# Two buffers instead of three for half tiles of the adjacency, and longer rings of masks, in a two-layer graph network kernel

## The chip, the cores and the metric

The kernel runs on one core of one Trainium2 chip. The metric is the device time of one execution in microseconds (us), the median of several runs.

## What is computed

The input is x (8192 nodes by 64 channels, f32) and adj (8192 by 8192, int32, 256 MB). Two graph layers follow each other.

```
h = relu(layernorm(x))                      # layer 0: two attention passes, mask = adj > 0
for i in range(2):
    Wh = h @ W[i];  u, v = vectors made of Wh and the attention weights
    e = leaky_relu(u + v.T + c)
    att = softmax(where(mask, e, -9e15), axis=1)
    h = 0.2 * h_input + 0.8 * elu(att @ Wh)
x = x + concat(h_input, h1, h2) @ mlp_w + mlp_b
h = relu(layernorm(x))                      # layer 1: mean over the neighbours, a = (adj == 1)
x = x + concat(a @ h / rowsum(a), h) @ weight + bias
```

The softmax is computed without exponentials of the whole matrix: exp(leaky_relu(u+v)) splits into a product of a row factor and a column factor on either side of the kink. So each attention pass needs, for each element of the adjacency, one bit "neighbour, on-side" (u+v above zero) and one bit "neighbour, off-side", and multiplies these two bit masks with scaled values of Wh.

## The kernel before, in words

**Tiles.** The rows are taken in 8 groups of 1024 and the columns in 8 chunks of 1024; one (group, chunk) pair is a tile, number n, 64 in all. In the first attention pass a tile comes from HBM as two half tiles of 128 x 4096 int32, 2 MB each (line L285, issued by SyncE, short SP, from its own queue), number m = 2n + h. The landing places are `adjb`, NA buffers of 16 KB per partition, and SP issues load m only when VectorE (DVE) has converted half tile m - NA (`sp.wait_ge(coded, m - NA + 1)`).

**The front of a tile.** DVE converts each half tile to bytes (`convert`, L850), packs two bits per element (`pack_pairs` L860 and L861, `pack` L865), TensorE (PE) transposes the packed bytes (L1491), ScalarE (ACT) takes them out of PSUM into one of NP = 4 buffers `pt` (L469) and stores them to HBM as `codes_d` (L473, 256 KB). DVE converts tile n + 3 while it makes the masks of tile n.

**The units.** A tile is used in four units q = 0..3. For each unit ACT computes a sign ramp into the ring `onb` of NS buffers (L461, two instructions). DVE turns it in place into the on-side mask (`on_mask`, L828) and makes the off-side mask into the ring `offb` of NO buffers (`off_mask`, L838). PE multiplies: 16 matmuls with the on mask (L1501), then 16 with the off mask (L1507). ACT's ramp for unit U waits for PE's on-side matmuls and for the off mask of unit U - NS; DVE's off mask for unit U waits for PE's off-side matmuls of unit U - NO.

**The passes.** Pass 0 reads the adjacency itself. Pass 1 reads the 256 KB codes back, and so does the last stage, the neighbour mean, in which DVE picks masks out of the codes into the same ring `onb` (`pick`, L1333) and PE multiplies them (L1714). Every engine's program is one fixed list written out in order; the waits are semaphores.

**DVE's order in pass 0.** For a tile n with no side work it is: on 0, on 1, off 0, convert(n+3, 0), off 1, on 2, convert(n+3, 1), off 2, on 3, pack_pairs, off 3, pack. In the first eight tiles of the pass the splitting of Wh is interleaved; in the first four or so tiles of each later group the row work of the group before.

**The start.** SP issues the loads of x, the weights, and then the half tiles. Between the half tiles its queue holds the stores of m0 (eight of 256 KB, L288) at places given by the table `STORES`; each waits for the projection's products. POOL issues the small vectors' stores and their broadcasts (`u_d`, L325; `ub`, L332), the stored h (L338) and m1 (L355).

**The region.** All of the above but u shares one 94 KB region per partition: `adjb` at 0, `code`, `packed`, `pt`, `onb` and `offb` behind it. The m0 products wait for their store in the region's last 16 KB (78 to 94 KB), where mask buffers lie too, so the first user of such a buffer waits for `m0_st`: an ACT ramp (unit NS - 2) and DVE's first off mask.

Of the kernel before, what the change touches and what calls it, by code (L numbers as in the profile page):

```python
# [11 lines left out]
U8 = mybir.dt.uint8  # L12
# [14 lines left out]
CHJ = 1024  # L27
# [5 lines left out]
NG = N // RG  # L33
# [16 lines left out]
HTOP = 4096.0  # L50
ROOT = 0x5F3759DF
SPLIT_ON, SPLIT_OFF, SPLIT_Y = 5, 3, 3
NA, NP, NS, NO = 3, 4, 8, 6
KB = 1024


def word(bits):
    return bits * 0x01010101


def w32(buf):
    return buf.bitcast(U32)
# [24 lines left out]
def gnn_program(nc, x, adj, w, lin_w, lin_b, attn, mlp_w, mlp_b, w1, bias1, out):  # L87
    ctx = ExitStack()
    with ctx:
# [3 lines left out]
        def sem(name):  # L93
            return ctx.enter_context(nc.semaphore(name))
# [56 lines left out]
        def at(off, n, dt):  # L151
            return region[:, off:off + n].bitcast(dt)

        adjb = [at(16 * i * KB, 16 * KB, I32).rearrange("p (t j) -> p t j", j=CHJ) for i in range(NA)]
        code = at(48 * KB, 8 * KB, U8).rearrange("p (t j) -> p t j", j=CHJ)
        packed = at(56 * KB, 2 * KB, U8)
        pt = [at(58 * KB + 2 * i * KB, 2 * KB, U8) for i in range(NP)]
        onb = [at(66 * KB + 2 * i * KB, 2 * KB, U8) for i in range(NS)]
        offb = [at(82 * KB + 2 * i * KB, 2 * KB, U8) for i in range(NO)]
        xq = [at(78 * KB + 4 * ((k + 1) % 4) * KB, 4 * KB, FP32).rearrange("p (t c) -> p t c", c=C) for k in range(4)]  # L160
        m0 = [at(78 * KB + 2 * ((k + 2) % 8) * KB, 2 * KB, FP32).rearrange("p (t c) -> p t c", c=C) for k in range(NG)]
        xi = [at(2 * i * KB, 2 * KB, FP32).rearrange("p (t c) -> p t c", c=C) for i in range(2)]
# [63 lines left out]
        m0_st, m_st = sem("m0_stored"), [sem(f"m1_stored{i}") for i in range(2)]  # L226
# [27 lines left out]
        o_r, o_st = sem("out_ready"), [sem(f"out_stored{i}") for i in range(2)]  # L254

        NWA, NWT = 16 * 6, 16 * 8
        STORES = {3: (0,), 4: (1, 2), 5: (3,), 6: (4, 5, 6, 7)}

        def nth(l, c):

# [6 lines left out]
        with nc.Block() as block:  # L267

            @block.sync
            def _(sp):  # L270
# [9 lines left out]
                for m in range(2 * NT):  # L280
# [4 lines left out]
                    sp.dma_start(adjb[m % NA], adj_v[g, h, :, :, c * CHJ:(c + 1) * CHJ]).then_inc(adj_in[m % NA], 16)  # L285
                    for k in STORES.get(m, ()):
                        sp.wait_ge(mm_out, 3 * k + 3)
# [109 lines left out]
            def _(act):  # L397
# [45 lines left out]
                def ramps(l, n, q):  # L443
                    U = LU * l + 4 * n + q
                    g, c = n // NCH, n % NCH
                    G = NG * l + g
                    if U >= NS:
                        act.wait_ge(on_done, U - NS + 1)
                        act.wait_ge(off_r, U - NS + 1)
                    elif U == NS - 2:  # L450
                        act.wait_ge(m0_st, 16 * NG)
                    if q == 0 and c == 0:
                        act.wait_ge(ub_in[G % 2], 16 * (G // 2 + 1))
                    if q == 0 and g == 0 and l == 0:
                        act.wait_ge(bv_r, 1)
                    if q == 0 and g == 0 and l == 1:
                        act.wait_ge(d_r, NG + c + 1)
                    sv = onb[U % NS].rearrange("k (i b) -> k b i", b=2)
                    for b in range(2):
                        t = c * TC + 2 * q + b  # L460
                        last = nc.scalar.activation(sv[:, b, :], ub[G % 2][:, :], ACT.Relu, bias=bigv[l][:, t:t + 1], scale=BIG)  # L461
                    last.then_inc(sgn, 1)
# [63 lines left out]
                for n in range(NT):  # L526
                    g, r = n // NCH, n % NCH
                    ramps(0, n, 0)
                    if g == 0 and r > 0:
                        cast_high(0, r)  # L530
                    ramps(0, n, 1)
                    if n + 1 < NT:
                        take_codes(n + 1)
                    if r == 5 and g > 0:
                        high(NG + g - 1)
                    ramps(0, n, 2)
                    if n + 1 < NT:
                        store_codes(n + 1)
                    if g == 0 and r > 0:
                        cast_middle(0, r)  # L540
                    ramps(0, n, 3)
                    if g > 0 and r == 7:
                        products(NG + g - 1, 0, tpb)
                    if g > 1 and r < 2:
                        products(NG + g - 2, r + 1, tpb)
                    if g > 0 and r == 0:
                        scaled_sums(g - 1)
                    if g > 0 and r == 3:
                        row_exp(g - 1)
                    if g > 0 and r == 6:  # L550
                        take_ht(NG + g - 1, tpb)
# [32 lines left out]
            def _(dve):  # L584
# [246 lines left out]
                def off_mask(l, n, q):  # L831
                    U = LU * l + 4 * n + q
                    if U >= NO:
                        dve.wait_ge(off_done, U - NO + 1)
                    elif U == 0:
                        dve.wait_ge(m0_st, 16 * NG)
                    dve.wait_ge(on_r, U + 1)
                    nc.vector.scalar_tensor_tensor(w32(offb[U % NO]), w32(pt[(NT * l + n) % NP]), word(BITS[q]), w32(onb[U % NS]),  # L838
                                                   ALU.bitwise_and, ALU.bitwise_xor).then_inc(off_r, 1)
# [174 lines left out]
                for n in range(NT):  # L1014
# [5 lines left out]
                    on_mask(0, n, 0)  # L1020
                    on_mask(0, n, 1)
                    off_mask(0, n, 0)
                    if n + 1 < NCH:
                        split_rest(0, n + 1)
                    if ahead:
                        convert(n + 3, 0)
                    off_mask(0, n, 1)
                    if g > 0 and r == 1:
                        add_pairs(g - 1)
# [17 lines left out]
                    if n == 1:  # L1047
                        h_spread(0)
                    off_mask(0, n, 2)
                    if g > 0 and r == 1:  # L1050
                        lonely_add(g - 1)
# [733 lines left out]
```

## Time and profile before

| quantity | us |
|---|---|
| median of 3 runs | 1757.43 (1756.73 to 1758.02) |
| the profiled execution | 1757.3 |
| its span, first to last instruction | 1755.5 |
| PE busy in the span | 1532.0 (87%) |
| DVE busy | 1539.7 (88%) |
| ACT busy | 1269.0 (72%) |
| DMA queue of SP, share of 16 engines | 46.9% |

The busy times are unions over the whole span, and the stages differ: pass 0 ends at about 865 us, pass 1 at about 1500 us, and the mean takes the rest. The shares above say little of any one stage, so the rows below are cut by stage.

### The profile page before, as it was taken

How to read it: one execution, taken by the hardware profiler on the slowest of the kernel's cores; microseconds unless marked ns; L12 is line 12 of the kernel's file. 1: busy time of each engine (PE TensorE's matmuls, PEld its weight loads, DVE VectorE, ACT ScalarE, POOL GpSimd, SP SyncE). 2: the span in 40 equal slices, each digit the busy share in tenths (PEclk: the TensorE clock that was granted, in tenths of full speed). 3: DMA queues.
4: the chain of work that ended last, by engine and by line, in shares of the span. 5: the costliest groups of instructions: out<-in, count | busy, mean ns of one | idle time of the engine just before them, and what ended most of it. 6: DMA issues, size and time to landing. Idle time of an engine off the chain costs nothing. (4 is left out here: it accounts for less than half of the span.)

```text
span 1755.5 us, 50261 instructions
## 1 busy us (share of the span) xinstructions
PE 1532.0 (87%) x21779; PEld 1483.6 (85%) x21779; DVE 1539.7 (88%) x2544; ACT 1269.0 (72%) x1404; POOL 82.7 (5%) x116
## 2 busy tenths in 40 slices
PE   2268888888988888888779999999999999799998
PEld 2267778787878878787779999999999999799998
DVE  7799999999999999999788878879688788986665
ACT  4668888888979989888689999999999995000000
POOL 1100000101000010101010000000000000000000
PEclk9689999999999999999989999999999999999999
DMA  7998999999999999998121112122121211233231
GB/s 248 263 363 322 374 359 393 355 409 361 406 379 386 389 378 402 353 409 317 37 68 44 56 43 56 44 68 57 43 62 44 56 50 31 61 112 90 86 93 43
DMA packets 115389, 356.02 MB, mean 203 GB/s; under 512 B 9184, under 2 KB 17376, under 8 KB 115168
## 3 DMA queue, kind: packets, MB, share of 16 engines
q1 hardware_dynamic: 92192, 306.37, 46.9%
q0 software_dynamic: 8512, 27.33, 5.8%
q10 hardware_dynamic: 14464, 19.11, 3.0%
q8 instruction: 171, 2.80, 0.7%
q14 instruction: 50, 0.41, 0.1%
HBM read 325.45 MB, written 27.33 MB: 201 GB/s over the span
## 5 line engine op out<-in xcount | busy, mean ns | idle before, releaser
L461 ACT ACTIVATE region<-ub,bigv 128x1024 uint8<-128x1024 f32 x1024 | 1096.0, 1152 | 28.6 <-PE bank L1507 11.2
L1501 PE MATMUL bank<-wsplit,region 128*128 128x195 bf16 x8192 | 779.3, 248 | 46.2 <-DVE region L828 37.3
L1501 PEld LDWEIGHTS bank<-wsplit,region 128*128 128x128 fp8e3 x8192 | 687.1, 98 | 58.4 <-DVE region L828 41.3
L1507 PE MATMUL bank<-wsplit,region 128*128 128x130 f16 x8192 | 556.6, 221 | 63.4 <-DVE region L838 62.3
L1507 PEld LDWEIGHTS bank<-wsplit,region 128*128 128x128 fp8e3 x8192 | 499.0, 98 | 92.8 <-DVE region L838 92.7
L838 DVE SCALAR_TENSOR_TENSOR region<-region 128x512 uint32<-128x512 uint32 x512 | 338.4, 680 | 10.9 <-PE bank L1507 8.7
L828 DVE SCALAR_TENSOR_TENSOR region<-region 128x512 uint32<-128x512 uint32 x512 | 334.2, 681 | 10.8 <-ACT region L461 10.7
L850 DVE TENSOR_SCALAR region<-region 128x4096 uint8<-128x4096 int32 x128 | 292.0, 2281 | 9.6 <-DMA region<-in_adj 9.6
L1714 PE MATMUL bank<-wsplit,region 128*128 128x129 f16 x4096 | 243.5, 222 | 11.2 <-DVE region L1333 11.2
L1714 PEld LDWEIGHTS bank<-wsplit,region 128*128 128x128 fp8e3 x4096 | 241.4, 99 | 12.4 <-DVE region L1333 12.4
L1333 DVE TENSOR_SCALAR region<-region 128x512 uint32<-128x512 uint32 x256 | 100.2, 424 | 43.2 <-PE bank L1714 37.4
L469 ACT ACTIVATE region<-bank 128x1024 uint16<-128x1024 uint16 x64 | 66.0, 1031 | 26.8 <-PE bank L1491 26.0
L493 ACT ACTIVATE po<-po 128x512 f32<-128x512 f32 x16 | 10.0, 626 | 85.3 <-DVE po L946 85.3
L1491 PE MATMUL bank<-identb,region 128*128 128x128 bf16 x512 | 40.6, 224 | 33.9 <-DVE region L865 23.3
L1491 PEld LDWEIGHTS bank<-identb,region 128*128 128x128 bf16 x512 | 32.4, 100 | 34.5 <-DVE region L865 23.7
L1459 PE MATMUL bank<-w,hT 128*128 128x130 f16 (+2 forms) x512 | 37.5, 224 | 19.8 <-ACT hT L418 9.5
L1459 PEld LDWEIGHTS bank<-w,hT 128*128 128x128 f16 x512 | 30.9, 103 | 22.1 <-issue 9.8
L325 POOL DMA_DIRECT2D u_d<-vu x16 | 12.1, 760 | 671.8 <-DVE vu L660 608.0
L1322 DVE SCALAR_TENSOR_TENSOR region<-region 128x512 uint32<-128x512 uint32 x64 | 43.6, 682 | 0.0
L860 DVE SCALAR_TENSOR_TENSOR region<-region 128x512 uint32<-128x512 uint32 x64 | 43.5, 679 | 0.1
L865 DVE SCALAR_TENSOR_TENSOR region<-region 128x512 uint32<-128x512 uint32 x64 | 43.5, 679 | 0.0
L861 DVE SCALAR_TENSOR_TENSOR region<-region 128x512 uint32<-128x512 uint32 x64 | 43.4, 679 | 0.0
(192 smaller groups left out, 689.8 us busy)
## 6 DMA issues: line engine op xcount, KB each, us to landing
region<-in_adj SPq DMA_DIRECT2D x128, 2048.0 KB, 10.8
region<-codes_d SPq DMA_DIRECT2D x128, 256.0 KB, 2.7
codes_d<-region ACTq DMA_DIRECT2D x64, 256.0 KB, 6.4
ub<-u_d POOLq DMA_DIRECT2D x16, 512.0 KB, 6.1
hg<-h_d POOLq DMA_DIRECT2D x16, 256.0 KB, 6.2
stg<-m_d POOLq DMA_DIRECT2D x16, 256.0 KB, 5.0
region<-in_x SPq DMA_DIRECT2D x4, 512.0 KB, 6.8
h_d<-wsplit POOLq DMA_DIRECT2D x4, 512.0 KB, 4.4
```

The lines of the kernel that those rows point to most:

```text
L461: last = nc.scalar.activation(sv[:, b, :], ub[G % 2][:, :], ACT.Relu, bias=bigv[l][:, t:t + 1], scale=BIG)
L469: nc.scalar.activation(pt[n % NP].bitcast(U16), tpb[:, :].bitcast(U16), ACT.Copy).then_inc(p_in, 1)
L828: nc.vector.scalar_tensor_tensor(on, on, word(BITS[q]), w32(pt[(NT * l + n) % NP]), ALU.bitwise_and, ALU.bitwise_and).then_inc(on_r, 1)
L838: nc.vector.scalar_tensor_tensor(w32(offb[U % NO]), w32(pt[(NT * l + n) % NP]), word(BITS[q]), w32(onb[U % NS]), ALU.bitwise_and, ALU.bitw ...
L850: nc.vector.tensor_scalar(code[:, 4 * h:4 * h + 4, :], adjb[m % NA], 1.375, 3.0, ALU.mult, ALU.min).then_inc(coded, 1)
L1322: nc.vector.scalar_tensor_tensor(w32(xb[i % 2]), m32, 1, m32, ALU.logical_shift_right, ALU.bitwise_xor).then_inc(mixed, 1)
L1333: nc.vector.tensor_scalar(w32(onb[V % NS]), w32(xb[i % 2]), word(BITS[q]), None, ALU.bitwise_and).then_inc(eq, 1)
L1459: last = nc.tensor.matmul(pb[:, k * width:(k + 1) * width], ht[:, it * P:(it + 1) * P], rhs(j), start=(k == 0 and j == 0), stop=(j == 1), ...
L1491: last = nc.tensor.transpose(tpb[:, :].bitcast(BF16)[:, it * P:(it + 1) * P], src[:, it, :], identb[:, :])
L1501: return nc.tensor.matmul(acc_on[it], columns(onb[U % NS], it, b), wsplit[:, c * TC + 2 * q + b, 0:WC], start=(c == 0 and q == 0 and b == ...
L1507: return nc.tensor.matmul(acc_off[it], columns(offb[U % NO], it, b), woff[:, c * TC + 2 * q + b, WO:WO + WF], start=(c == 0 and q == 0 and ...
L1714: last = nc.tensor.matmul(acc_m[g % 2][it], columns(onb[V % NS], it, b), wf16[:, c * TC + 2 * q + b, :], start=(first and b == 0 and it % ...
```

## The change

`adjb` gets two buffers in place of three, which frees 16 KB per partition. The ring of on-side masks grows from 8 to 12 buffers and that of off-side masks from 6 to 10. The region is laid out anew, and what hangs on the number of buffers moves with it: SP's load m waits for the conversion of m - 2; the m0 stores stand one load earlier in SP's queue; the wait for these stores leaves ACT's ramp and goes from DVE's off mask 0 to off mask 2, the first whose buffer lies in the m0 area. No instruction that computes is added or removed.

```
-NA, NP, NS, NO = 3, 4, 8, 6
+NA, NP, NS, NO = 2, 4, 12, 10
...
-        code = at(48 * KB, 8 * KB, U8).rearrange("p (t j) -> p t j", j=CHJ)
-        packed = at(56 * KB, 2 * KB, U8)
-        pt = [at(58 * KB + 2 * i * KB, 2 * KB, U8) for i in range(NP)]
-        onb = [at(66 * KB + 2 * i * KB, 2 * KB, U8) for i in range(NS)]
-        offb = [at(82 * KB + 2 * i * KB, 2 * KB, U8) for i in range(NO)]
+        code = at(32 * KB, 8 * KB, U8).rearrange("p (t j) -> p t j", j=CHJ)
+        packed = at(40 * KB, 2 * KB, U8)
+        pt = [at(42 * KB + 2 * i * KB, 2 * KB, U8) for i in range(NP)]
+        onb = [at(50 * KB + 2 * i * KB, 2 * KB, U8) for i in range(NS)]
+        offb = [at(74 * KB + 2 * i * KB, 2 * KB, U8) for i in range(NO)]
...
-        STORES = {3: (0,), 4: (1, 2), 5: (3,), 6: (4, 5, 6, 7)}
+        STORES = {2: (0,), 3: (1, 2), 4: (3,), 5: (4, 5, 6, 7)}
...
                     if U >= NS:
                         act.wait_ge(on_done, U - NS + 1)
                         act.wait_ge(off_r, U - NS + 1)
-                    elif U == NS - 2:
-                        act.wait_ge(m0_st, 16 * NG)
...
                     if U >= NO:
                         dve.wait_ge(off_done, U - NO + 1)
-                    elif U == 0:
+                    elif U == 2:
                         dve.wait_ge(m0_st, 16 * NG)
```

## Rows read from the trace of the kernel before

**Rows 1.** Windows: busy us per engine, PEclk, DMA share, GB/s; pass 0, pass 1.
```profile
98.00:833.00 735.00, 621.44 (x8334) 580.82 (x8332) 734.25 (x924) 628.25 (x734) 28.09 (x25) 0.99 0.97 374
1000.00:1400.00 400.00, 400.00 (x5715) 400.00 (x5713) 319.58 (x598) 376.36 (x353) 20.87 (x30) 1.00 0.18 53
```
**Rows 2.** Waits in 98 to 833: us in total, times, longest.
```profile
PE bank L1507 <- DVE region L838: 60.4, 80, 1.9
PE bank L1501 <- DVE region L828: 34.8, 32, 2.9
```
**Rows 3.** Waits of DVE and PE after 865: us in total, times, longest.
```profile
DVE region L838 <- PE bank L1507: 8.7, 8, 1.6
PE bank L1714 <- DVE region L1333: 11.2, 7, 4.2
```
**Rows 4.** The conversions (L850), by source: durations in ns, waits on DMA.
```profile
L850 DVE TENSOR_SCALAR region<-region x128: 2273/2281/2294, 43.1 to 831.4; 128x4096 uint8<-128x4096 int32 x128
  DMA region<-in_adj: 9.6, 3
```
**Rows 5.** Timeline of DVE, 371 to 388, conversions only: start, us.
```profile
371.90 2.28 DVE L850 TENSOR_SCALAR region<-region 128x4096 uint8<-128x4096 int32 x1
375.31 2.28 DVE L850 TENSOR_SCALAR region<-region 128x4096 uint8<-128x4096 int32 x1
382.93 2.28 DVE L850 TENSOR_SCALAR region<-region 128x4096 uint8<-128x4096 int32 x1
386.33 2.28 DVE L850 TENSOR_SCALAR region<-region 128x4096 uint8<-128x4096 int32 x1
```
**Rows 6.** The half tile load issued at 230.8, by tile: issue to landing.
```profile
L285 SPq DMA_DIRECT2D region<-in_adj x1: 367/367/367, 230.8 to 230.8; - x1
DMA to landing us min/median/max: 7.4/7.4/7.4
```
**Rows 7.** Windows: the DMA around an idle gap, and two later stretches.
```profile
138.80:141.00 2.20, 2.20 (x35) 2.20 (x33) 2.20 (x3) 1.33 (x2) 0.00 (x0) 1.00 0.00 0
141.00:143.00 2.00, 2.00 (x31) 2.00 (x29) 2.00 (x2) 2.00 (x3) 0.00 (x0) 1.00 0.85 207
366.00:372.00 6.00, 5.49 (x77) 5.07 (x75) 6.00 (x11) 5.46 (x7) 0.00 (x0) 1.00 1.03 412
337.00:343.00 6.00, 5.30 (x69) 4.67 (x67) 6.00 (x6) 6.00 (x7) 2.35 (x1) 1.00 1.03 212
```
**Rows 8.** Timeline of POOL and DVE, 334 to 355: a group's small transfers, the conversions.
```profile
334.68 0.77 POOL L325 DMA_DIRECT2D u_d<-vu  x1 [146.98 <-DVE vu L660]
336.99 2.37 POOL L332 DMA_DIRECT2D ub<-u_d  x1
...
336.95 2.28 DVE L850 TENSOR_SCALAR region<-region 128x4096 uint8<-128x4096 int32 x1
340.96 2.28 DVE L850 TENSOR_SCALAR region<-region 128x4096 uint8<-128x4096 int32 x1
...
349.18 2.28 DVE L850 TENSOR_SCALAR region<-region 128x4096 uint8<-128x4096 int32 x1
...
352.59 2.28 DVE L850 TENSOR_SCALAR region<-region 128x4096 uint8<-128x4096 int32 x1
```
**Rows 9.** Timeline of DVE, 38 to 98: conversions with their idle time, off mask 0.
```profile
57.65 2.29 DVE L850 TENSOR_SCALAR region<-region 128x4096 uint8<-128x4096 int32 x1 [2.02 <-DMA region<-in_adj]
...
72.93 2.29 DVE L850 TENSOR_SCALAR region<-region 128x4096 uint8<-128x4096 int32 x1 [4.99 <-DMA region<-in_adj]
...
84.67 2.29 DVE L850 TENSOR_SCALAR region<-region 128x4096 uint8<-128x4096 int32 x1 [2.55 <-DMA region<-in_adj]
...
92.91 0.69 DVE L838 SCALAR_TENSOR_TENSOR region<-region 128x512 uint32<-128x512 uint32 x1 [1.48 <-DMA m_d<-region]
```
**Rows 10.** Windows: the start, before and while the transfers queue up.
```profile
31.00:45.00 14.00, 7.51 (x96) 7.22 (x96) 9.55 (x14) 11.57 (x29) 3.33 (x4) 1.00 0.26 97
60.00:76.00 16.00, 3.00 (x19) 2.12 (x19) 10.09 (x38) 9.65 (x12) 2.59 (x4) 0.50 1.06 158
```

## The prediction

> **What bounds the kernel now.** I read the windows first, because the two kinds of buffer that trade places here serve different stages. In pass 0, from 98 to 833 us, DVE is busy 734.25 of 735.00 us, PE 621 and ACT 628 [rows 1]. That is one engine at its limit with nothing to give. The DMA share in the same row is 0.97 at a mean of 374 GB/s, so the transfers are a close second. In pass 1, PE is busy 400.00 of 400 us and DVE only 320; nothing there waits for the adjacency [rows 1].
>
> The waits say the same. In pass 0 PE waits 60.4 us for off masks and 34.8 us for on masks [rows 2]: its backlog is short or empty, so a microsecond in which DVE stands still is a microsecond of the pass. DVE itself waits for loads of the adjacency only three times, 9.6 us in all [rows 4], and all three are in the start [rows 9]. With three buffers the loads are hidden for the whole of the steady part. Whether two still hide them is the question.
>
> **The deeper rings.** They can only help where a mask maker waits for a free buffer while PE starves. In pass 0 DVE has no idle time to recover [rows 1]. In pass 1 DVE does wait for PE to free off masks, 8.7 us in all [rows 3], but PE is at 100% there, so earlier masks are masks that wait longer. At the change to the mean stage PE waits 11.2 us for picks [rows 3]; those come from DVE's row work between the picks, in a written order that stays, and DVE, not the ring, is late. I cost the rings at nothing. Bounds: no gain, and at most the 11.2 us.
>
> **The loads, steady part.** A half tile is 2048 KB, 2.10 MB; at the 412 GB/s of a queue kept full [rows 7] it takes 5.09 us. A tile moves two of them and one store of codes of 256 KB, together 4.46 MB or 10.8 us. A tile without side work lasts 382.93 - 371.90 = 11.03 us on DVE, and its two conversions start 3.41 us apart [rows 5]. So such a tile uses 98% of what the engines can move, and no gap may be left between transfers.
>
> With three buffers load m is issued when conversion m - 3 ends, with two when conversion m - 2 ends. Take the tile at 371.90. The first buffer is free at 371.90 + 2.28 = 374.2 and its load is issued then. A load that finds the engines idle lands 7.4 us later [rows 6]: 381.6, in time for 382.93. The second, issued at 377.6, queues behind it and behind the codes: 381.6 + 5.1 + 0.6 = 387.3, wanted at 386.33. It is 1.0 us late. The delay does not pay fully each time: with x the distance between the two conversions of a tile, the period is x + 7.62 (the rest of the tile), the second load lands 2.3 + 7.4 + 5.7 = 15.4 us after the tile began, and this must equal period + x. So x = 3.9 against 3.41, and a tile costs 0.5 us more.
>
> Bounds of it: if a load is always queued before the one ahead of it ends, a tile needs only 10.8 us and the cost is 0; if every tile pays the whole lateness it is 1.0. The trace shows both parts of the 7.4 us. After an idle gap of 2.2 us the first 2.0 us of the next load move only 207 GB/s [rows 7], which loses (412 - 207)/412 x 2.0 = 1.0 us at the front of the transfer. The next load would be issued at most a microsecond before the one ahead of it lands, so sometimes the gap opens and sometimes not. I take the 0.5 of the lone load, the nearest row.
>
> The Trainium skill, page "DMA: Bandwidth & Descriptors", section "Anatomy of one DMA", puts a fixed cost of about 2.0 us on each DMA and says that most of it is the receipt after the last byte. The total agrees with this trace (7.4 less 5.1 is 2.3 us). By that rule the engines are already done two microseconds before a landing, so a gap would open in every tile and the 0.5 us would be certain; by the slow first microseconds of the window at 141 about half of the fixed part sits at the front and vanishes whenever a load is queued, which would make the cost nearer 0.1 to 0.3.
>
> In the steady part I count 26 intervals of 11.03 us like that in [rows 5], and 7 of 11.6 to 11.7 us, whose second load by the same sum is 0.4 us late and costs 0.2. The other 27 last 12.2 us or more and have room, which the next paragraph uses up in some of them. Sum: 26 x 0.5 + 7 x 0.2 = 14.4 us. Bounds 0 and 28.
>
> **The loads beside a group's small transfers.** Once in each group from the third on, POOL issues four transfers in a row [rows 8]: u, m1, h0 and the broadcast of u. While they run the engines are full but move only 212 GB/s, from 337 to 343 us [rows 7]. With three buffers a half tile was in flight all that time, and the worst load still came 1.1 us early (its conversion at 352.59 did not wait). With two, the load for 349.18 is issued at 336.95 + 2.3 = 339.3 and the one for 352.59 at 343.3. Nothing of either moves before about 343. Then two loads and a store of codes follow: 343 + 10.2 + 0.6 + 0.3 to land = 354.1, and up to 354.9 with a slow front. Wanted is 352.59: 1.5 to 2.3 us late, I take 2.0. There are six such places in pass 0: 12 us. Bounds 0 (the small transfers finish beside the loads as before) and 4 each, 24.
>
> **The start.** Three half tiles land before the first conversion at 43.1 [rows 4]; from 31 to 45 the engines move only 97 GB/s [rows 10] because all three buffers are full. With two, the third half tile must come after 45 instead, in the stretch in which DVE already waits 2.02, 4.99 and 2.55 us for loads [rows 9] and the queue is at a share of 1.06 [rows 10]. Every later landing moves by one transfer, 5.1 us. Against it stands the wait of off mask 0 for the m0 stores, 1.48 us [rows 9]: now off mask 2 has that wait, about 10 us later, and the stores, whose place in the queue is one load earlier, are in by then. ACT's ramp 6 loses a wait that delayed nobody whom the trace shows. Moved in SP's queue are eight store issues and one load issue of about 0.4 us each; SP has nothing else to do. One risk is larger: the second conversion of tile 1, at 57.65, stands in DVE's list ahead of the last projection results, and its load is now the one that landed at 72.9. At worst it holds the chain that leads to the conversion at 72.93 by some 15 us. I take 5.1 - 1.5 = 4 us; bounds 2 and 15.
>
> **Sum.** 14.4 + 12 + 4 - 0 = 30 us. The profiled execution took 1757.3 us, 1.8 more than its span of 1755.5 and 0.1 from the median of 1757.43. So 1787 us.
>
> **Rivals.**
> - *The transfers stay hidden.* For it: the short tile needs 10.8 of 11.03 us, and loads with another one in flight lose nothing at the front. Against it: 0.2 us of room in a tile, and the room of three buffers was down to 1 us at the group's small transfers. Then only the start is left: 1757.3 + 4 = 1761.
> - *The engines' gap opens in every tile and the small transfers hit full.* 28 + 24 + 15 = 67 us: 1824. For it: the queue already runs at 98%, and the stores of codes share the engines. Against it: the upper bounds all at once.
> - *The rings pay.* One mechanism on the other side: PE's 11.2 us of waits for picks go, because a ring of 12 lets DVE run four picks further ahead of its row work. It decides only if loads stay hidden, for at 30 us of stalls it can't turn the sign. 1757.3 + 4 - 11 = 1750. Against it: before the first pick DVE waits for pass 1's sums, and no depth moves that.
> - *The edit does not bind.* The start's transfer hides in the slack of the first tiles, which last over 14 us, and the rest stays hidden: 1757 to 1759.
>
> **How the numbers follow.** Forecast 0.70; all stalls at their bounds 0.13; transfers hidden but for the start 0.09; no change 0.05; the rings pay 0.03. The likeliest gives 1787 us. Its own range is 1768 (14.4 and 12 at a third, start at 2) to 1808 (about 1.7 times the sum). Toward the cases at either side I widen it to 1761 to 1816. About 0.2%, 3.5 us, is what a measurement of this kernel tells from no change. The hidden case at 1761 lies just above that bound and counts as slower: slower 0.92, same 0.05, faster 0.03.
>
> **What would show it.** In the profile after, the conversions' group should have gained idle time before it with the landing of the adjacency as releaser: about 25 to 40 us against 9.6, and dozens of times against three. Pass 0's window should show DVE with some 25 us idle where it has 0.75, the DMA's GB/s lower than 374, and short tiles of 11.3 to 11.6 us. At each group's small transfers a stall of about 2 us should stand before the second conversion. Issue to landing should fall below the median of before, since fewer loads are in flight. Pass 1 and the mean should last as long as before, to 2 us. It is wrong if the conversions' idle time stays near 10 us, if the loss lies in the start alone, or if PE's waits for picks shrink by more than a few microseconds.

## The result

| | us |
|---|---|
| before, median of 4 runs | 1757.56 (1756.73 to 1758.02) |
| after, median of 4 runs | 1822.82 (1822.37 to 1825.11) |
| ratio, 95% interval | 1.0372 (1.0358 to 1.0385) |
| span of the profiled execution after | 1823.3 |

The changed kernel is 65 us slower. The forecast was 30 us slower, with 59 as the end of its range: the sign and the mechanism came out, the size did not.

**Where the time went.** The windows of the kernel after, shifted so that they hold the same work as those of [rows 1] (columns: stretch, its length, busy us of PE, weight loads, DVE, ACT, POOL, then PEclk, DMA share, GB/s):

```profile
102.00:900.00 798.00, 648.16 (x8327) 609.08 (x8324) 738.45 (x923) 632.41 (x738) 28.08 (x25) 0.94 0.92 345
1066.00:1466.00 400.00, 400.00 (x5714) 400.00 (x5712) 318.79 (x598) 372.41 (x360) 20.87 (x30) 1.00 0.19 54
```

Pass 0 takes 798 us in place of 735. DVE does the same work (738 against 734 us) and now stands still for 60 us. Pass 1 is as before: PE at 100%, DVE 319 of 400 us. The DMA engines move the same bytes in both windows, at a share of 0.92 in place of 0.97. That is 0.92 x 798 = 734 us busy against 713, and 64 us idle against 22. So some 42 us are engines with nothing to do, and some 21 us are engines at work, but slower. Loads come too late: DVE's only waits in this window are for them. TensorE's granted clock is not the cause, though its mean fell from 0.99 to 0.94 and PE's busy time rose from 621 to 648 us: DVE, which sets the pace here, waits for PE nowhere in the window. The conversions by source, and the waits of pass 0 and of the change to the mean stage (us in total, times, longest), to be read against [rows 2 to 4]:

```profile
L848 DVE TENSOR_SCALAR region<-region x128: 2278/2284/2509, 43.1 to 897.9; 128x4096 uint8<-128x4096 int32 x128
  DMA region<-in_adj: 73.2, 43
```
```profile
PE bank L1505 <- DVE region L836: 83.8, 73, 4.4
DVE region L848 <- DMA region<-in_adj: 58.9, 41, 3.4
PE bank L1499 <- DVE region L826: 45.7, 28, 6.0
...
PE bank L1712 <- DVE region L1331: 10.9, 7, 4.2
```

DVE waits 73.2 us for half tiles in 43 places, where it waited 9.6 in three. PE's waits for masks grow from 60 and 35 us to 84 and 46. PE's wait for picks, the one thing that longer rings could have taken away, is 10.9 us against 11.2.

**The same waits, one by one.** I summed the idle time before each of the 128 conversions by where it stands:

| place | before | forecast | after |
|---|---|---|---|
| start (tiles 0 to 3), waits | 9.6 | | 14.6 |
| shift of the conversion at 109.0 | | 4 | 3.9 |
| short tiles | 0 | 14.4 | 34.0 in 26 places |
| six groups' small transfers | 0 | 12 | 24.7 |
| PE waits for picks | 11.2 | 11.2 | 10.9 |

The start is right. Two terms are twice as large as forecast or more. The three terms add up to 62.6 of the 65 us.

**A short tile after.** DVE's timeline, conversions only, and the loads for the last two of them. This is one of the dearer tiles: behind the 26 intervals of 11.03 us the second conversion waited from 0 to 3.3 us, 1.07 on average. The loads are shown by SP's issue, then us from issue to landing; [rows 5, 6] are their counterparts:

```profile
393.05 2.29 DVE L848 TENSOR_SCALAR region<-region 128x4096 uint8<-128x4096 int32 x1
398.28 2.29 DVE L848 TENSOR_SCALAR region<-region 128x4096 uint8<-128x4096 int32 x1 [1.74 <-DMA region<-in_adj]
405.91 2.28 DVE L848 TENSOR_SCALAR region<-region 128x4096 uint8<-128x4096 int32 x1
410.96 2.29 DVE L848 TENSOR_SCALAR region<-region 128x4096 uint8<-128x4096 int32 x1 [1.57 <-DMA region<-in_adj]
```
```profile
L285 SPq DMA_DIRECT2D region<-in_adj x1: 367/367/367, 395.4 to 395.4; - x1
DMA to landing us min/median/max: 8.6/8.6/8.6
...
L285 SPq DMA_DIRECT2D region<-in_adj x1: 368/368/368, 400.6 to 400.6; - x1
DMA to landing us min/median/max: 10.3/10.3/10.3
```

The first load lands 8.6 us after its issue, at 404.0, and not 7.4. The second lands at 400.6 + 10.3 = 410.9, 6.9 us after the first, and not 5.7. The tile lasts 405.91 - 393.05 = 12.9 us against 11.03. Where those microseconds are lost is seen in the windows around the same tile:

```profile
396.50:398.50 2.00, 2.00 (x33) 2.00 (x32) 0.26 (x2) 2.00 (x4) 0.00 (x0) 1.00 1.05 324
400.00:402.00 2.00, 0.77 (x14) 0.78 (x15) 2.00 (x4) 2.00 (x3) 0.00 (x0) 1.00 1.03 418
407.50:410.50 3.00, 2.74 (x38) 2.33 (x35) 1.89 (x3) 3.00 (x4) 0.00 (x0) 1.00 0.74 247
```

In the middle of a load the engines move 418 GB/s. From 396.5 to 398.5 the load ahead ends (the conversion at 398.28 waits for it) and the one issued at 395.4 begins: 324 GB/s, with a share of 1.05, so the engines are all busy, but slower. From 407.5 to 410.5 the second load ends, and the next one was issued only at 408.2: 247 GB/s at a share of 0.74. A store of codes runs in both stretches. The kernel before has 410 to 412 GB/s through a whole tile [rows 7].

Both kernels have the next load issued before the one ahead lands; what differs is how long before. Here the loads of 395.4 and 400.6 went 2.9 and 3.4 us before the landing ahead of them. In the kernel before those of 374.2 and 377.6 went 4.9 and 6.6 us before it, and it keeps its rate.

**A group's small transfers after**, conversions of DVE, against [rows 8]:

```profile
353.03 2.28 DVE L848 TENSOR_SCALAR region<-region 128x4096 uint8<-128x4096 int32 x1
357.48 2.29 DVE L848 TENSOR_SCALAR region<-region 128x4096 uint8<-128x4096 int32 x1 [0.37 <-DMA region<-in_adj]
366.81 2.30 DVE L848 TENSOR_SCALAR region<-region 128x4096 uint8<-128x4096 int32 x1 [1.02 <-DMA region<-in_adj]
373.73 2.29 DVE L848 TENSOR_SCALAR region<-region 128x4096 uint8<-128x4096 int32 x1 [3.43 <-DMA region<-in_adj]
```

Not only the second conversion of the later tile is late, but three, 4.8 us in all.

### The profile page after: what moved, and what is told of

Its sections match the earlier page's. It is cut to its first block and busy times, and to the rows that moved or that the text cites. A ratio compares the mean times of both kernels' runs of the same rounds, so it can differ in the third digit from the quotient of the medians.

```text
span 1823.3 us, 50253 instructions
## 1 busy us (share of the span) xinstructions
PE 1561.2 (86%) x21779; PEld 1515.0 (83%) x21779; DVE 1538.8 (84%) x2544; ACT 1256.9 (69%) x1404; POOL 82.4 (5%) x116
## 5 line engine op out<-in xcount | busy, mean ns | idle before, releaser
L459 ACT ACTIVATE region<-ub,bigv 128x1024 uint8<-128x1024 f32 x1024 | 1082.8, 1149 | 9.5 <-PE bank L1505 5.7
L1499 PE MATMUL bank<-wsplit,region 128*128 128x195 bf16 x8192 | 803.9, 253 | 56.3 <-DVE region L826 47.6
L1499 PEld LDWEIGHTS bank<-wsplit,region 128*128 128x128 fp8e3 x8192 | 707.2, 100 | 71.0 <-DVE region L826 50.9
L1505 PE MATMUL bank<-wsplit,region 128*128 128x130 f16 x8192 | 565.6, 223 | 87.8 <-DVE region L836 86.9
L1505 PEld LDWEIGHTS bank<-wsplit,region 128*128 128x128 fp8e3 x8192 | 509.7, 99 | 112.2 <-DVE region L836 111.7
L848 DVE TENSOR_SCALAR region<-region 128x4096 uint8<-128x4096 int32 x128 | 293.0, 2289 | 73.5 <-DMA region<-in_adj 73.2
L826 DVE SCALAR_TENSOR_TENSOR region<-region 128x512 uint32<-128x512 uint32 x512 | 334.7, 682 | 11.8 <-ACT region L459 11.7
L836 DVE SCALAR_TENSOR_TENSOR region<-region 128x512 uint32<-128x512 uint32 x512 | 338.4, 681 | 0.7
L1712 PE MATMUL bank<-wsplit,region 128*128 128x129 f16 x4096 | 243.7, 222 | 10.9 <-DVE region L1331 10.9
L1712 PEld LDWEIGHTS bank<-wsplit,region 128*128 128x128 fp8e3 x4096 | 241.6, 99 | 12.2 <-DVE region L1331 12.1
L1331 DVE TENSOR_SCALAR region<-region 128x512 uint32<-128x512 uint32 x256 | 96.2, 422 | 22.2 <-PE bank L1712 17.1
L1489 PEld LDWEIGHTS bank<-identb,region 128*128 128x128 bf16 x512 | 32.5, 100 | 34.0 <-issue 17.8
L480 ACT ACTIVATE parts<-bank,rowf 128x195 f32<-128x195 f32 x56 | 20.3, 420 | 45.0 <-PE bank L1499 45.0
L858 DVE SCALAR_TENSOR_TENSOR region<-region 128x512 uint32<-128x512 uint32 x64 | 43.7, 682 | 0.1
L863 DVE SCALAR_TENSOR_TENSOR region<-region 128x512 uint32<-128x512 uint32 x64 | 43.6, 681 | 0.0
L1320 DVE SCALAR_TENSOR_TENSOR region<-region 128x512 uint32<-128x512 uint32 x64 | 43.6, 682 | 0.0
```

The source lines that it names most:

```text
L826: nc.vector.scalar_tensor_tensor(on, on, word(BITS[q]), w32(pt[(NT * l + n) % NP]), ALU.bitwise_and, ALU.bitwise_and).then_inc(on_r, 1)
L848: nc.vector.tensor_scalar(code[:, 4 * h:4 * h + 4, :], adjb[m % NA], 1.375, 3.0, ALU.mult, ALU.min).then_inc(coded, 1)
L858: nc.vector.scalar_tensor_tensor(pk, cq[1], 2, cq[0], ALU.logical_shift_left, ALU.bitwise_or).then_inc(pairs_r, 1)
L1331: nc.vector.tensor_scalar(w32(onb[V % NS]), w32(xb[i % 2]), word(BITS[q]), None, ALU.bitwise_and).then_inc(eq, 1)
L1489: last = nc.tensor.transpose(tpb[:, :].bitcast(BF16)[:, it * P:(it + 1) * P], src[:, it, :], identb[:, :])
L1499: return nc.tensor.matmul(acc_on[it], columns(onb[U % NS], it, b), wsplit[:, c * TC + 2 * q + b, 0:WC], start=(c == 0 and q == 0 and b == ...
```

## The experiments

Each was run beside the kernel before, which then took 1759.8 to 1760.5 us, some 3 us more than beside the kernel after; so the ratios are what to compare. "Waits" are DVE's waits for half tiles in pass 0 without the start (58.9 us in 41 places in the kernel after, of them 0.3 at the end of the start; none before). The code lines of the profiles shift by a few with each edit.

### E1 and E2: is it the rings, the layout, or when loads are issued?

E1 is the kernel before with only the issue rule of two buffers, and with the m0 stores one load earlier, as they go in the kernel after.

```
-                    if m >= NA:
-                        sp.wait_ge(coded, m - NA + 1)
+                    if m >= 2:
+                        sp.wait_ge(coded, m - 1)
...
-        STORES = {3: (0,), 4: (1, 2), 5: (3,), 6: (4, 5, 6, 7)}
+        STORES = {2: (0,), 3: (1, 2), 4: (3,), 5: (4, 5, 6, 7)}
```

> The kernel before, its three buffers, rings and layout kept, but SP issues half tile m only when half tile m - 2 is converted, and the m0 stores stand one load earlier. Theory A (the whole loss is when loads are issued; rings and layout are worth nothing): ratio to before 1.035 to 1.040, some 1820 to 1825 us, the conversions idle about 73 us for loads. Rival B (the longer rings or the new layout cost part of it, for instance through ACT running further ahead): the rule alone gives what the prediction had, 1785 to 1800 us, ratio 1.016 to 1.024.

E2 is the kernel after with the old rings.

```
-NA, NP, NS, NO = 2, 4, 12, 10
+NA, NP, NS, NO = 2, 4, 8, 6
...
-        offb = [at(74 * KB + 2 * i * KB, 2 * KB, U8) for i in range(NO)]
+        offb = [at(82 * KB + 2 * i * KB, 2 * KB, U8) for i in range(NO)]
...
-                    elif U == 2:
+                    elif U == 0:
                         dve.wait_ge(m0_st, 16 * NG)
```

> The changed kernel with two buffers, but with rings of 8 and 6 again (on-side masks right behind the codes, off-side masks at 82 KB; off mask 0 waits for the m0 stores). Theory A: 1820 to 1825 us, the same as the changed kernel within 3 us. Rival B (longer rings cost): 1785 to 1800 us. Rival C (longer rings give back a part that the stalls would else cost): 1828 us or more.

E1: 1823.7 us, ratio 1.0360 (1.0344 to 1.0375), waits 59.9 us. E2: 1822.9 us, ratio 1.0355 (1.0339 to 1.0370), waits 54.4 us. The issue rule alone, with three buffers still there, gives the whole loss. The rings, alone on top of it or left out, change nothing that can be measured. Rivals B and C fall. The longer rings with three buffers were not tried: the region of 94 KB has no room for both. What they would be worth there stays open.

### E3 and E5: the spacing of the two conversions

```
                     on_mask(0, n, 0)
+                    if ahead:
+                        convert(n + 3, 0)
                     on_mask(0, n, 1)
                     off_mask(0, n, 0)
...
-                    if ahead:
-                        convert(n + 3, 0)
                     off_mask(0, n, 1)
...
                     on_mask(0, n, 2)
-                    if ahead:
-                        convert(n + 3, 1)
...
                     off_mask(0, n, 2)
...
+                    if ahead:
+                        convert(n + 3, 1)
                     on_mask(0, n, 3)
```

E3 has this in the kernel after, E5 in the kernel before.

> The changed kernel with DVE's two conversions of a tile moved apart: convert 0 behind on mask 0, convert 1 ahead of on mask 3. Their starts are then about 5.2 us apart and 5.8 us from the next in place of 3.4 and 7.6. Theory A1 (the second load is late because it is issued 3.4 us behind the first and then the queue runs to its end once a tile): the stalls of the short tiles all but go, the conversions idle 5 to 25 us (the start and the groups' small transfers), 1765 to 1785 us. Rival D (with two buffers every load pays its fixed part, however they are spaced): the conversions idle over 50 us still, 1805 us or more.

> The kernel before, three buffers, with the conversions moved apart as in the run with two. Control for the order of DVE's list. If the order itself costs nothing, 1757 to 1760 us; then the 54 us that the two-buffer version with this order is still above the kernel before are all loads. If it costs, for instance in the first eight tiles where the splitting of Wh waits on ACT, 1764 to 1772 us, and the loads' part there is 42 to 48 us.

E3: 1813.5 us, ratio 1.0304 (1.0285 to 1.0323). E5: 1766.5 us, ratio 1.0038 (1.0023 to 1.0053). By its numbers E3 went to Rival D: 1805 us or more, and the conversions idle 53.4 us in all. By the place of the waits it did not. The short tiles' waits fell from 34.0 to 7.6 us, as Theory A1 had it:

```profile
309.00 2.28 DVE L848 TENSOR_SCALAR region<-region 128x4096 uint8<-128x4096 int32 x1
314.48 2.29 DVE L848 TENSOR_SCALAR region<-region 128x4096 uint8<-128x4096 int32 x1
320.30 2.28 DVE L848 TENSOR_SCALAR region<-region 128x4096 uint8<-128x4096 int32 x1
...
364.56 2.29 DVE L848 TENSOR_SCALAR region<-region 128x4096 uint8<-128x4096 int32 x1 [4.09 <-DMA region<-in_adj]
370.24 2.29 DVE L848 TENSOR_SCALAR region<-region 128x4096 uint8<-128x4096 int32 x1 [0.18 <-DMA region<-in_adj]
```

A tile without side work now runs in 320.30 - 309.00 = 11.3 us and waits for nothing. But the groups' places kept theirs (27.5 us), the start waits 18.6, and E5 shows that the order itself costs 6.6 us. What two buffers cost in this order is E3 less E5, 47 us.

### E4: fewer bytes

```
-                    sp.dma_start(pt[M % NP], codes_d[n]).then_inc(c_in[M % NP], 16)
+                    sp.dma_start(pt[M % NP], codes_d[n % 4]).then_inc(c_in[M % NP], 16)
...
-                act.dma_start(codes_d[n], pt[n % NP]).then_inc(c_st[n % NP], 16)
+                act.dma_start(codes_d[n] if n < 4 else codes_d[n][0:16, 0:128],
+                              pt[n % NP] if n < 4 else pt[n % NP][0:16, 0:128]).then_inc(c_st[n % NP], 16)
```

> The changed kernel, but from tile 4 on ACT stores only 2 KB of the 256 KB of codes, and the later passes read the codes of tiles 0 to 3 again (as many bytes as before). A short tile then moves 4.19 MB, 10.2 us at 412 GB/s, in 11.03. Theory A1 (slow fronts after the queue has run to its end): the stall of a short tile falls by about half of the 0.65 us that the store takes, and the loss shrinks to some 45 us, 1795 to 1810 us. Rival E (the engines are at 98% of their rate and that alone is it): with 8% of room nearly all stalls of the short tiles go, 1780 us or less.

E4: 1811.1 us, ratio 1.0289 (1.0274 to 1.0304), waits 43.4 us; the short tiles keep 22.7 of 34.0. With 8% of room in the rate of the engines, two thirds of the short tiles' loss stay. Rival E falls: want of rate alone does not make the loads late; for the larger part it is when they may go. The time came out just above my range for A1.

### E7, E8 and E10: what in a group's small transfers delays the loads

E7 replaces the broadcast read, E8 the store of u, E10 cuts u, m1 and h0 down together.

```
# E7: as many bytes, 128 different rows, for groups 3 to 7
+    pool.dma_start(ub[G % 2][:, :], u_d[...].partition_broadcast(P) if G < 3 or G >= NG else h0_d[:, 0:RG])
...
# E8 and E10: u of pass 1
+    pool.dma_start(u_d[1, 16 * k:16 * k + 16].rearrange("(p b) -> p b", b=1), vu[0:16, 1, 0:1])
...
# E10 only
+    pool.dma_start(dgrp(m1_d, e)[0:16, 0, :], xg[X % 2][0:16, 0, :])
+    pool.dma_start(hg[E % 2][0:16, 0, :], dgrp(h0_d, E % NG)[0:16, 0, :])
```

> The changed kernel, but for groups 3 to 7 of pass 0 the 512 KB that fill ub are 128 different rows of h0 in place of one row of u read 128 times (the values are wrong, the masks differ, the amount of work does not). Theory G1 (the slow six microseconds beside each group's small transfers come from the broadcast read): the stalls there fall from 4 us to under 2 each, 5 of the 6 places, and the time to 1808 to 1813 us. Rival G2 (they come from the store of u in 8-byte pieces or from the sum of the four): within 3 us of 1823.

> The changed kernel, but in pass 0 the store of u for pass 1 writes 16 values in place of 1024 in 8-byte pieces, and pass 1 reads the u of pass 0. Theory G2 (the store in small pieces makes the slow microseconds): the groups' stalls fall from 25 us to under 12, the time to 1808 to 1813 us. Rival G1 or G3 (the broadcast read, or simply the 1.3 MB of the four transfers): within 4 us of 1823.

> The changed kernel, but in pass 0 three of the four small transfers of a group (u, m1 and h0) move 16 rows of 256 bytes or less; the broadcast of u stays, and later stages read other data in their place, as many bytes. Theory G3 (a group's stall is the time that its 1.3 MB take from an engine queue with no reserve): the groups' stalls fall from 25 to 5 to 12 us, the short tiles keep theirs, 1804 to 1812 us. Rival G4 (the stall there comes from where the loads are issued and not from the four transfers): the stalls stay above 18 us, 1815 us or more.

E7: 1827.9 us, ratio 1.0386 (1.0367 to 1.0404), groups' waits 30.8 us. E8: 1820.4 us, 1.0353 (1.0334 to 1.0372), 22.4 us. E10: 1813.4 us, 1.0306 (1.0289 to 1.0323), 14.2 us. In the kernel after, E1 and E2, which do the same there, the groups' waits are 24.7, 27.6 and 24.8 us, so neither E7 nor E8 shows a gain that stands out. It is not that the broadcast reads one row 128 times, nor the small pieces of u alone; three of the transfers together carry 10.5 of the 24.7 us. The rest is still there with only the broadcast beside the loads. No run takes the broadcast's 512 KB away, so whether the rest is theirs or comes from when the loads may go stays open. E10's waits fell between the two theories' ranges and its time just above G3's.

What POOL's queue takes of the engines can be read, though. Packets, MB and the share of 16 engines, from 300 to 860 us, five groups' transfers, in the kernel after, E7, E8 and E10:

```profile
q0 software_dynamic: 1680, 5.26, 4.7%
q0 software_dynamic: 1680, 5.26, 5.4%
q0 software_dynamic: 1680, 5.24, 3.0%
q0 software_dynamic: 1200, 2.66, 1.6%
```

Of 560 us that is 26 us of all engines in the kernel after and 17 in E8. The 4 KB of u, in 8-byte pieces, account for a good third of what the 1 MB of a group's four transfers costs, near 2 us a group. That is a part of the slow stretch of [rows 7]; it is not what makes the conversions late, for without it the waits stayed at 22.4 us.

### E6, E9 and E12: more loads in the queue

E6 cuts the same 32 KB into four buffers of quarter tiles; E12 has five of them (40 KB) and rings of 10 and 8; E9 is the kernel before with the later issue for the second half tile only.

```
# E6
-NA, NP, NS, NO = 2, 4, 12, 10
+NA, NP, NS, NO = 4, 4, 12, 10
...
-        adjb = [at(16 * i * KB, 16 * KB, I32)...
+        adjb = [at(8 * i * KB, 8 * KB, I32)...
...
-                for m in range(2 * NT):
+                for m in range(4 * NT):
...
# E9
-                        sp.wait_ge(coded, m - NA + 1)
+                        sp.wait_ge(coded, m - NA + 1 + m % 2)
```

> The changed kernel, but its 32 KB of landing space are four buffers for quarter tiles (1 MB each) in place of two for half tiles; two conversions of 2048 columns stand where one of 4096 stood. Up to four loads can be queued, so the queue seldom runs to its end, and each load is free to go 1.1 us earlier. Theory A2 (the loss of the short tiles is the engines standing idle or starting slowly between loads): that loss falls from 34 us to under 10, the groups' 25 us stay at 15 to 25, and the doubled conversions add some 5 to 8 us of DVE: 1785 to 1800 us. Rival F (what counts is the space, 32 KB, not how it is cut): 1820 us or more.

> The kernel before with three buffers, but the second half tile of a tile (odd m) is issued only when half tile m - 2 is converted, as with two buffers; the first half tile (even m) still goes when m - 3 is converted. The two loads of a tile boundary are then issued together. Theory A3 (what costs is that the queue holds at most one load beyond the one under way, so it runs out or restarts once a tile): with the pair issued together the engines are fed, the short tiles wait under 10 us in all, and only the groups' places and the start cost something: 1765 to 1785 us. Rival H (each load that is late by the two-buffer rule costs by itself): half of the loss, 1790 us or more.

> Five buffers of quarter tiles (40 KB) in place of four (32 KB), rings of 10 and 8. Against the run with four quarter buffers (1796 us): if the loss falls steadily with the landing space, half of the loads' share goes, 1775 to 1783 us. If the space has a threshold at about what the engines need, nearly all goes but the start and the doubled conversions, 1765 to 1772 us.

| | time | ratio (95%) | waits, steady part |
|---|---|---|---|
| after | 1822.8 | 1.0372 (1.0358, 1.0385) | 58.9 in 41 |
| E6, four quarters | 1795.8 | 1.0209 (1.0194, 1.0225) | 23.6 in 21 |
| E9, one half late | 1783.9 | 1.0148 (1.0125, 1.0172) | 18.8 in 16 |
| E12, five quarters | 1775.5 | 1.0088 (1.0074, 1.0102) | 3.6 in 3 |

E6 and E9 came out as Theories A2 and A3 had it. The same 32 KB in four pieces take away 35 of the 59 us of waits; the short tiles keep 4.2 us. Another 8 KB take away nearly all that is left. E12's time is that of the steady fall (1775 to 1783 us), but its waits are those of the threshold. Pass 0 of E12 as one window, to be read against that of the kernel after above, and its waits:

```profile
102.00:853.00 751.00, 638.19 (x8363) 598.53 (x8361) 746.56 (x1050) 633.24 (x738) 23.96 (x25) 0.97 0.97 366
```
```profile
DVE region L849 <- DMA region<-in_adj: 3.6, 3, 1.5
```

The DMA share is back at 0.97, and DVE stands still for 4 us of 751. What E12 still pays is DVE's. One part is the start: tile 4 begins at 114.6 us in place of 109.0. The other is the doubled conversions: a short tile lasts 11.16 us in place of 11.03. E9 shows how little it takes: with the first half tile of each tile issued as early as with three buffers, two loads stand in the queue together, and two thirds of the waits are gone.

### E11: a better start for the kernel before

```
-        onb = [at(66 * KB + 2 * i * KB, 2 * KB, U8) for i in range(NS)]
-        offb = [at(82 * KB + 2 * i * KB, 2 * KB, U8) for i in range(NO)]
+        onb = [at(k * KB, 2 * KB, U8) for k in (66, 68, 70, 72, 82, 84, 86, 88)]
+        offb = [at(k * KB, 2 * KB, U8) for k in (74, 76, 78, 80, 90, 92)]
...
-        STORES = {3: (0,), 4: (1, 2), 5: (3,), 6: (4, 5, 6, 7)}
+        STORES = {5: (0, 1, 2, 3), 6: (4, 5, 6, 7)}
...
-                    elif U == NS - 2:
+                    elif U == 4:
                         act.wait_ge(m0_st, 16 * NG)
...
-                    elif U == 0:
+                    elif U == 2:
                         dve.wait_ge(m0_st, 16 * NG)
```

> The kernel before, three buffers and rings of 8 and 6, but the slots of the two rings are shared out so that off mask 0 needs none of the m0 area (off mask 2 and ramp 4 wait for the stores instead), and the stores of m0 stand behind half tiles 5 and 6. The wait of 1.48 us before off mask 0 goes, and the loads for the conversions at 72.93 and 84.67 come up to 1.3 and 2 us earlier: 1754 to 1756 us, 0.1 to 0.2% faster. Rival (the start is held by the slow stretch of the engines at 60 to 76 us, whatever the order): no change.

E11: 1762.9 us, ratio 1.0016 (1.0008 to 1.0025). It missed: it is slower by 0.16%. Its waits between 60 and 115 us point at a cause:

```profile
ACT region L461 <- DMA m_d<-region: 18.7, 1, 18.7
DVE region L850 <- DMA region<-in_adj: 8.5, 2, 5.9
DVE bb L815 <- ACT wsplit L498: 6.1, 1, 6.1
```

The wait for the m0 stores, moved to ACT's ramp 4, holds ACT for 18.7 us, and behind it in ACT's list stands the cast that DVE needs. Which share of the loss is this wait's and which is the later stores', no run separates. Nothing in these runs beats the kernel before.

## Why the prediction was wrong, step by step

- **What bounds the kernel**: right. Pass 0 is DVE's, each stall of DVE is a stall of the pass (waits up by 64 us; time by 65 in the medians, by 68 in the profiled executions), and pass 1 did not move.
- **The rings at nothing**: right for two buffers, shown by E1 and E2 and by PE's wait for picks (10.9 against 11.2 us); with three buffers no run has longer rings.
- **The start, 4 us**: right in sum, 3.9 us at the conversion at 109.0. Its parts moved too: the second conversion of tile 1 waits 9.8 us for its load, the risk that the prediction named; the later waits shrink for it.
- **The steady part, 14.4 us**: this is the step that failed first. It measured 34.0 us, above even its upper bound of 28. The 26 intervals of 11.03 us, priced at 0.5 each and at most 1.0, cost 1.07 on average; they do not all cost the same, behind five of them there was no wait. The equation for the period holds in the tile shown: 2.3 + 8.6 + 6.9 = 17.8 us, and the observed period and distance are 17.9 together. What went into it was too small. The 7.4 us of [rows 6] is the shortest of all loads of the steady part, and the load behind the idle gap of [rows 7], issued at 140.2 into engines at rest, took 9.5 in the same trace (loads from 98 to 833 us, then that one; below them the windows from its issue on):

```profile
L285 SPq DMA_DIRECT2D region<-in_adj x118: 367/368/368, 100.5 to 818.1; - x118
DMA to landing us min/median/max: 7.4/10.6/15.0
...
L285 SPq DMA_DIRECT2D region<-in_adj x1: 367/367/367, 140.2 to 140.2; - x1
DMA to landing us min/median/max: 9.5/9.5/9.5
```
```profile
140.20:141.20 1.00, 1.00 (x17) 1.00 (x15) 1.00 (x2) 1.00 (x2) 0.00 (x0) 1.00 0.00 0
141.20:143.20 2.00, 2.00 (x31) 2.00 (x29) 2.00 (x2) 2.00 (x4) 0.00 (x0) 1.00 0.96 252
```

  The 5.7 us came from a queue that is never empty [rows 7]. The prediction held that a load issued before the one ahead lands, if only by up to 1 us, loses little at the front, and used the slow start at 141 us to argue the cost down. The loads of the kernel after were issued 2.9 and 3.4 us before that landing and were slow all the same. Part of it is seen in the windows: for 1.0 us after an issue nothing moves, and the two microseconds after that are slow. Here a load had to be issued well before the landing ahead to keep the rate, not just before it.
- **The groups' small transfers, 12 us**: mis-sized, 24.7. The place and the order of events were right. I priced one late conversion of 2.0 us; the trace has two or three late ones, 3.5 to 4.9 us a place. That nothing can be issued ahead to catch up is my reading of it; E10 shows that 10.5 us of it belong to three of the four transfers.
- **The rival "the gap opens in every tile"**, 1824 us at 0.13, came within 2 us of the time, but partly by luck: its 28, 24 and 15 us measured 34.0, 24.7 and 3.9, so an error in the start hid one in the tiles. Nor did a gap open in every tile. What it had right is that the steady part and the groups are both dear. I held it unlikely because it needed all upper bounds at once. But the bounds were not independent: one cause, too little in reserve, moves the steady part and the groups together. A range made of terms with a common cause must be as wide as the terms together.
- **The receipt rule of the Trainium skill** ("DMA: Bandwidth & Descriptors", section "Anatomy of one DMA") was set beside the trace's split of the 7.4 us as the case in which the tile's cost is certain. That section describes transfers issued by GpSimd; these loads are SP's. It spoke against my lower figures, and the measured cost was larger than either. The trace agrees with it in the total of the fixed part, but does not bear out that most of it comes after the last byte: behind the issue at 140.2 a window of 1.0 us passes before anything moves, and the front of the load is slow after that. How much comes behind the last byte the windows don't show.

## What to carry to other kernels

A landing buffer is a place in the DMA queue. Before one is given up, add up per period what must be moved at the measured rate (here 10.8 of 11.03 us) and look at how long before the landing ahead each load could then be issued: here 4.9 us kept the queue's full rate and 3.4 us did not. If the space is needed elsewhere, cut it finer before cutting it down: the same 32 KB as four quarters in place of two halves ran 27 us faster (29 by the ratios), for all that they double the conversions.

## What was not expected of the hardware

- Where one load ends and the next starts late, the engines move 207 to 324 GB/s over two or three microseconds, against 410 to 420 in the middle of a load, at shares of 0.74 to 1.05 [rows 7 and the windows above]. At 1.05 they are not idle but slow.
- Nothing moves for the first 1.0 us after the load of 140.2 is issued to engines at rest.
- The DMA engines' idle share in pass 0 rose from 3% to 8%, and the same bytes took 21 us more of busy time besides.
- A store of 4 KB in 8-byte pieces takes near 2 us of all 16 engines (26 against 17 us in five groups, the kernel after and E8).
- A conversion of 2048 columns takes 1.22 us and one of 4096 takes 2.28, but they overlap a little with what follows: a tile with its two conversions cut into four costs 0.13 us more (11.16 against 11.03), where 2 x 1.22 less 2.28, twice, would be 0.32.
